# State-space layer: skip term by a diagonal matrix on TensorE, logarithm with the one as bias, second projection ahead of a round

## What is computed

```python
x = einsum('bld,ed->bel', hidden_states, in_proj_w)          # 4 x 256 channels x 256 tokens
x = silu(depthwise causal conv of 4 taps over x + conv_b)     # this is u
dt_low, Bm, Cm = split(einsum('bdl,ed->bel', x, x_proj_w), [8, 24])
dt = softplus(einsum('brl,dr->bdl', dt_low, dt_proj_w) + dt_proj_b)
A = -exp(A_log)                                               # 256 x 16
def step(state, d, b, c, u):                                  # along the tokens
    state = state * exp(d * A) + (d * u) * b
    y = einsum('bdn,bn->bd', state, c)
y = (y + D * x) * silu(z)                                     # D * x is the skip term
```

## Time and profile before

| | us |
|---|---|
| median of 3 runs | 1440.1 |
| lowest and highest of them | 1439.5, 1444.04 |
| time of the profiled execution | 1443.76 |
| its span, first to last instruction | 1442.0 |
| TensorE busy | 1310.5 (91%) |
| VectorE busy | 1019.6 (71%) |
| ScalarE busy | 706.4 (49%) |
| GpSimd busy | 272.7 (19%) |
| mean granted TensorE clock | 0.950 of full |

### The profile page before, as it was taken

How to read it: one execution, slowest core, us unless ns; L and a number is a source line. 1 busy time by engine, 2 the same in 40 slices (tenths; PEclk the granted TensorE clock), 3 DMA queues, 4 the chain that set the end, 5 groups by cost and what they waited for, 6 DMA issues and landing times.

```text
span 1442.0 us, 20925 instructions
## 1 busy us (share of the span) xinstructions
PE 1310.5 (91%) x6697; PEld 920.2 (64%) x6697; DVE 1019.6 (71%) x2264; ACT 706.4 (49%) x1825; POOL 272.7 (19%) x258
## 2 busy tenths in 40 slices
PE   7898699989996668999999789987999999989998
PEld 3455465663342355766776789976888888765555
DVE  6999877988986877778777522236666666667665
ACT  5797524444774847455554112225666666623110
POOL 0787310010000003222220371111111111201000
PEclk8899889999998879999999699998999999989999
DMA  6579600044502000010105488855222221101330
GB/s 224 169 252 318 206 2 0 0 74 76 89 10 85 0 0 1 1 37 1 37 1 146 168 314 309 305 191 191 74 73 73 74 78 66 36 1 48 82 92 29
DMA packets 83570, 141.80 MB, mean 98 GB/s; under 512 B 45606, under 2 KB 57327, under 8 KB 78528
## 3 DMA queue, kind: packets, MB, share of 16 engines
q1 hardware_dynamic: 80528, 134.44, 29.5%
q0 software_dynamic: 1872, 4.22, 0.8%
q10 hardware_dynamic: 1088, 2.10, 0.4%
HBM read 105.32 MB, written 26.37 MB: 91 GB/s over the span
## 4 chain that ended last, share of the span: by engine, by line
PE 74%; DVE 12%; ACT 5%; issue 3%; DMA 3%; POOL 2%; SPq 1%; DVEq 0%; POOLq 0%; ACTq 0%
PE psum L3363 5%; PE psum L2540 4%; PE psum L2106 4%; PE psum L2860 4%; PE psum L996 4%; PE psum L2912 4%; PE psum L2890 4%; PE psum L2148 4%; PE psum L2925 3%; PE psum L3373 3%; PE psum L603 2%; PE psum L537 2%; DVE roomB L1662 2%; PE psum L2138 2%; PE psum L2551 2%
## 5 line engine op out<-in xcount | busy, mean ns | idle before, releaser
L2982 ACT ACTIVATE roomA<-psum,roomA 128x256 f32<-128x256 f32 x128 | 70.9, 559 | 87.2 <-DVE roomA L3049 86.9
L2203 ACT ACTIVATE roomA<-psum,roomA 128x128 f32<-128x128 f32 (+1 forms) x128 | 53.2, 426 | 84.3 <-DVE roomA L2278 84.2
L1662 DVE TENSOR_REDUCE roomB<-psum 128x2 f32<-128x512 f32 x128 | 81.3, 685 | 10.5 <-PE psum L1501 10.0
L2711 DVE SCALAR_TENSOR_TENSOR roomA<-roomA,psum 128x512 f32<-128x512 f32 x23 | 15.9, 689 | 100.6 <-ACT roomA L2600 100.5
L2069 POOL TENSOR_TENSOR roomA<-roomA 128x512 f32<-128x512 f32 x40 | 51.1, 1279 | 176.6 <-DVE roomA L2271 176.6
L902 POOL TENSOR_TENSOR roomA<-roomA 128x1024 f32<-128x1024 f32 (+1 forms) x33 | 74.8, 2268 | 25.6 <-DVE roomA L822 24.9
L2106 PE MATMUL psum<-own,roomB 128*128 128x512 f32 x160 | 75.0, 594 | 3.4 <-DVE roomA L2270 2.1
L822 DVE TENSOR_TENSOR_SCAN roomA<-roomA,psum 128x512 f32<-128x512 f32 x64 | 74.3, 1200 | 0.9 <-ACT roomA L704 0.9
L3363 PE MATMUL psum<-roomA,roomB 128*112 128x512 f32 (+1 forms) x168 | 74.6, 593 | 0.0
L2912 PE MATMUL psum<-roomA 128*128 128x256 f32 x256 | 67.5, 386 | 1.7 <-ACT roomA L2990 0.7
L2890 PE MATMUL psum<-roomA 128*128 128x256 f32 x256 | 65.6, 379 | 1.7 <-ACT roomA L2982 1.7
(11 more groups left out here) (525 smaller groups left out, 3374.3 us busy)
## 6 DMA issues: line engine op xcount, KB each, us to landing
roomB<-m_w_dram SPq DMA_DIRECT2D x12, 1536.0 KB, 8.2
roomA<-m_w_dram SPq DMA_DIRECT2D x11, 1536.0 KB, 8.8
roomA<-m_c_rows SPq DMA_DIRECT2D x32, 512.0 KB, 4.6
a_kv_ready<-roomB SPq DMA_DIRECT2D x28, 512.0 KB, 5.3
roomA<-a_kv_ready SPq DMA_DIRECT2D x8, 1024.0 KB, 4.9
roomA<-a_kv_ready SPq DMA_DIRECT2D x16, 512.0 KB, 4.3
roomB<-a_w_dram SPq DMA_DIRECT2D x4, 1280.0 KB, 5.6
roomB<-f_w_dram SPq DMA_DIRECT2D x8, 624.0 KB, 4.3
```

The source lines that it names most:

```text
L1662: dve.tensor_reduce(maxneg[:, hp // 8, :, m, hp % 8], g.bank(m).rearrange("p (q k) -> p q k", k=S), AX.X, ALU.max, negate=True).then_inc(s ...
```

## The change

1. The skip term. Two 128x128 tiles `skips`, the identity times D, are made by VectorE at the start. `skip_over(j)` multiplies them with u on TensorE into banks 0 and 1, ahead of the first `add` of each half; the adds then all accumulate. `with_skip` is gone, `gate` reads PSUM, and for j = 0 both gates stand between product and scan of step 17.
2. The logarithm. `logarithm(j)` reads exp(-|v|) itself and takes a tile of ones as bias. `one_more(1)` goes from GpSimd to VectorE, at step 1 ahead of `remainder(1)`; `remainder(j)` now waits for the logarithm too, since it overwrites what that reads.
3. The order. `project(1)` stands ahead of round 4, whose halves stand behind it and behind `step_size(1)`. `kv_out(4)` moves from before the table load to behind `logarithm(1)`, ahead of `kv_out(5)`.

```diff
+        pool.memset(g.one, 1.0)
...
+    skips = ra.take(E2, P)
...
         project(0)
-        kv_round(4)
         pe.wait_ge(s["m_u"], 2)
         project(1).then_inc(s["m_dtlow_psum"], 1)
+        kv_round(4, range(0, 2))
         pe.wait_ge(s["m_kv_copied"], 4)
         pe.wait_ge(s["m_dtlow"], 1)
         step_size(0)
         pe.wait_ge(s["m_less"], 1)
         take_off(0)
         step_size(1)
+        kv_round(4, range(2, 4))
         take_off(1)
         for r in range(5, AHEAD):
             kv_round(r)
...
+        def skip_over(j):
+            pe.wait_ge(s["m_made"], 4)
+            pe.wait_ge(*((s["m_hc"], 1), (s["m_gated"], 1))[j])
+            for half in range(2):
+                pe.matmul(g.bank(Y_BANK + half), skips[:, j, :], u[:, j, half * HALF:(half + 1) * HALF],
+                          start=True, stop=False, skip_group_check=True)
+
         def add(k):
+            if k % NS == 0:
+                skip_over(k // NS)
             for half in range(2):
...
-                if k == NS:
-                    pe.wait_ge(s["m_gated"], 1)
                 pe.matmul(g.bank(Y_BANK + half), g.ident, hC[:, k % 2, half * HALF:(half + 1) * HALF],
-                          start=(k % NS == 0), stop=(k % NS == NS - 1), skip_group_check=True).then_inc(s["m_added"], 1)
+                          start=False, stop=(k % NS == NS - 1), skip_group_check=True).then_inc(s["m_added"], 1)
 
         def back(j):
-            pe.wait_ge(s["m_gated"], 2 + j)
+            pe.wait_ge(s["m_gated"], 1 + j)
...
         kv_out(3)
-        kv_out(4)
         act.preload_act_table_set(LN_EXP)
...
         def logarithm(j):
-            act.wait_ge(s["m_w"], j + 1)
-            act.activation(th[:, j, :], dtu[:, j, :], ACT.Ln).then_inc(s["m_ln"], 1)
+            act.wait_ge(s["m_e"], j + 1)
+            act.activation(th[:, j, :], e[:, j, :], ACT.Ln, bias=g.one).then_inc(s["m_ln"], 1)
...
         shrink(1)
         decay(1)
         logarithm(1)
+        kv_out(4)
         kv_out(AHEAD - 1)
...
+        for j in range(E2):
+            dve.tensor_scalar(skips[:, j, :], g.ident, skip[:, j:j + 1], None, ALU.mult).then_inc(s["m_made"], 1)
...
         def remainder(j):
             dve.wait_ge(s["m_w"], j + 1)
+            dve.wait_ge(s["m_ln"], j + 1)
...
-        def with_skip(j, half):
-            of = slice(half * HALF, (half + 1) * HALF)
+        def gate(j, half):
             dve.wait_ge(s["m_added"], 2 * NS * (j + 1) - 1 + half)
-            return dve.scalar_tensor_tensor(dtu[:, j, of], u[:, j, of], skip[:, j:j + 1], g.bank(Y_BANK + half), ALU.mult, ALU.add)
-
-        def gate(j, half):
-            y = by_seq(dtu[:, j, :])[:, 2 * half:2 * half + 2, :]
-            return dve.scalar_tensor_tensor(y, gates[:, 2 * half:2 * half + 2, j, :], 0.5, y, ALU.mult, ALU.mult)
+            y = g.bank(Y_BANK + half).rearrange("p (b l) -> p b l", b=2)
+            return dve.scalar_tensor_tensor(by_seq(dtu[:, j, :])[:, 2 * half:2 * half + 2, :], gates[:, 2 * half:2 * half + 2, j, :], 0.5, y,
+                                            ALU.mult, ALU.mult)
 
         for k in range(STEPS):
             inputs(k)
             if k == 1:
+                one_more(1)
                 remainder(1).then_inc(s["m_w"], 1)
             if k == NS + 1:
-                with_skip(0, 0)
-                with_skip(0, 1).then_inc(s["m_gated"], 1)
+                dve.wait_ge(s["m_gates"], 4)
+                gate(0, 0)
+                gate(0, 1).then_inc(s["m_gated"], 1)
             scan(k)
...
-            if k == NS + 2:
-                dve.wait_ge(s["m_gates"], 4)
-                dve.wait_ge(s["m_gated"], 1)
-                gate(0, 0)
-                gate(0, 1).then_inc(s["m_gated"], 1)
...
         for half in range(2):
-            step(with_skip(1, half))
             gate(1, half).then_inc(s["m_gated"], 1)
...
-        pool.wait_ge(s["m_e"], 2)
-        pool.tensor_scalar(dtu[:, 1, :], e[:, 1, :], 1.0, None, ALU.add).then_inc(s["m_w"], 1)
```

More of the change, by code:

```diff
@@ L600, in add @@
                     pe.wait_ge(s["m_hc"], k + 1 + (half if k == STEPS - 2 else k // (STEPS - 1)))
-                if k == NS:
-                    pe.wait_ge(s["m_gated"], 1)
                 pe.matmul(g.bank(Y_BANK + half), g.ident, hC[:, k % 2, half * HALF:(half + 1) * HALF],
-                          start=(k % NS == 0), stop=(k % NS == NS - 1), skip_group_check=True).then_inc(s["m_added"], 1)
+                          start=False, stop=(k % NS == NS - 1), skip_group_check=True).then_inc(s["m_added"], 1)
         def back(j):
-            pe.wait_ge(s["m_gated"], 2 + j)
+            pe.wait_ge(s["m_gated"], 1 + j)
             for i in range(NT):
                 if j and i == NT // 2:
-                    pe.wait_ge(s["m_gated"], 4)
+                    pe.wait_ge(s["m_gated"], 3)
                 b, r = i // 2, i % 2
@@ L653, in scalar @@
         act.activation(A, a_log, ACT.Exp).then_inc(s["m_aexp"], 1)
-        act.wait_ge(s["m_pad"], 2)
+        act.wait_ge(s["m_made"], 2)
         for b in range(4):
@@ L689, in scalar @@
         split(1)
-        act.wait_ge(s["m_u"], 2)
         logarithm(0)
@@ L728, in vector @@
         step = g.dve_steps
-        dve.memset(xpad[:, :, :, 0:TAPS - 1], 0.0).then_inc(s["m_pad"], 1)
+        dve.memset(xpad[:, :, :, 0:TAPS - 1], 0.0).then_inc(s["m_made"], 1)
         dve.wait_ge(s["ident"], 3)
@@ L733, in vector @@
         dve.tensor_copy(sel[0:96], ones[0:96, 0:NS].unsqueeze(2).to_broadcast([96, NS, P])).then_inc(s["m_sel"], 1)
-        dve.memset(by_seq(dA[1])[:, :, 0:1], 0.0).then_inc(s["m_pad"], 1)
+        dve.memset(by_seq(dA[1])[:, :, 0:1], 0.0).then_inc(s["m_made"], 1)
         dve.wait_ge(s["m_weights"], 48)
         step(dve.tensor_scalar(small[:, 0:10], small[:, 0:10], 0.5, None, ALU.mult))
+        for j in range(E2):
+            dve.tensor_scalar(skips[:, j, :], g.ident, skip[:, j:j + 1], None, ALU.mult).then_inc(s["m_made"], 1)
         def conv(j, k):
@@ L3646, in sb @@
             return Room(ctx.enter_context(nc.sbuf_tensor(name, [P, words], F32)), words)
-        own = sb("own", 2 * NT * D + KD * TOK + TOK + P + P // 2 + 240 + 256)
+        own = sb("own", 2 * NT * D + KD * TOK + TOK + P + P // 2 + 240 + 256 + 2)
         g.X = own.take(NT, D)
@@ L3661, in program @@
         g.var, g.rstd, g.t8a, g.t8b = (own.take(NT) for _ in range(4))
+        g.one = own.take(1)
         g.roomA = sb("roomA", 25600)
```

## The result

| | before | changed |
|---|---|---|
| median of the runs, us | 1440.26 (6 runs) | 1449.21 (6 runs) |
| lowest and highest, us | 1439.5, 1444.04 | 1447.72, 1452.9 |
| profiled execution, us | 1443.76 | 1447.72 |
| its span, us | 1442.0 | 1446.0 |

The ratio is 1.0065, 95% interval 1.0049 to 1.0081: the change makes the kernel slower by 9 us. The forecast was 1443.7, with a range up to 1447.5. Yet the two profiled executions lie 4.0 us apart, which is nearly the +3.6 of the forecast's sum. Both have to be explained.

The account below looks back on a forecast made before the run. VectorE was taken to pace the first layer's loop, TensorE close behind, after a TensorE-ScalarE prologue chain. 7.0 - 0.3 + 1.6 - 0.4 - 3.0 - 1.3 = +3.6 on median 1440.1 gave 1443.7 us, range 1438.5 to 1447.5.

Parts of the forecast that it names:

- first product at 47.3 instead of 40.3: Loop entry: VectorE's first product waits for round 4's deferred copy, round 5 and the first spread; loss 7.0 us.
- Second projection ahead of round 4: Prologue: projection starts at 22.45 instead of 23.50, dtlow copy at 24.45 instead of 25.93; 1.5 us gained there.
- Copy of round 4 behind the second logarithm, round 5, spread: Prologue: the chain the first product waits for; copy done at 43.0, round 5 from 43.05, first product 47.3.
- Logarithm with the one as bias: Prologue and step 1: remainder's wait hidden; second addition 0.7 us on VectorE, first product with C freed, gain 0.3.
- First skip pair: Ahead of the first add, partly at low clock: loss 1.6 us, of which 0.4 may be caught again.
- Gate of step 18 gone, end of the layer: Mid-loop a 3.43 us gate goes, gain 3.0; at the end two operations go, gain 1.3 us.
- the 0.4 that was to be caught again: First ten loop steps: half of a 0.85 us difference between ScalarE's and VectorE's delays regained, bounds 0 and 0.85.
- the clock staying up through the prologue: Rival: 2.4 GHz kept through the prologue, first product at 45.15, +4.8 instead of +7.0; 1441.5 us; chance 0.22.
- The C rows: Rival: C rows, queued behind round 4's store, reach GpSimd late, up to 1.5 us slip; 1445.2 us; chance 0.28.
- The chance of slower: Whole kernel: probability 0.37 that the change is measurably slower, against 0.53 within and 0.10 faster.
- The size of a measurable difference: Whole kernel: 0.3%, 4.3 us, taken as about what a measurement can tell from none.

Follow-up runs that it names:

- the order undone: Changed kernel with the second projection, round 4 and its copy back in the order of before; median 1440.69 us, ratio 0.9991.
- the skip term alone: Kernel before with only the skip term moved to TensorE and the gates reading PSUM; median 1441.76 us, ratio 0.9997.
- copy early: Changed kernel with ScalarE's copy of round 4 moved right behind the first logarithm; median 1440.44 us, ratio 0.9997.
- round 5 later: Changed kernel with round 5 moved behind the spread for step 1, copy of round 4 left in place; median 1450.43 us, ratio 1.0049.

## Why the prediction was wrong, step by step

**The step that failed** is the last of the sum: "The profiled execution took 1443.8 ... it lies 3.7 above the median of the three runs, and against the median 1440.1 the forecast is 1443.7". It carries a difference worked out in one execution over to the median, as if the 3.7 us lay outside the change's reach. They lay in it: by the traces 2.8 of them were the late first product (40.3 against 37.5), behind the late load of x, and the change takes out just that dependence. So the term "first product at 47.3 instead of 40.3" is not 7.0 but 9.8. Of the 2.8 the small copy's start is 1.5 (25.93 against 24.40), which the forecast booked as the projection's gain; the rest is that the first step sizes still ran at the full clock for a part or all of the way (2.55 and 1.95 us instead of 3.37), which it booked as the change's too. The forecast's other terms unchanged, the sum is then 9.8 - 0.3 + 1.6 - 0.4 - 3.0 - 1.3 = +6.4, near the 6.5 to 7.3 by which the adds to X move between the usual executions. The medians of the runs differ by 7.9 and 9.0 us; the cause of the last 0.6 to 2.5 us isn't shown.

Against the trace that it was made from the forecast held, in its parts too: spans +4.0 for +3.6, the first product 6.9 later for 7.0, 2.7 won back for 3.4, and the same time behind the adds to X (1275.8 against 1276.0).

Point by point:
- *Second projection ahead of round 4*: said 1.5 gained; measured 1.5 against the first trace, nothing against the usual one.
- *Copy of round 4 behind the second logarithm, round 5, spread*: right in every link, and shown by the copy moved and by the order undone.
- *Logarithm with the one as bias*: hidden, as said. The remainder began at 32.01 (31.9 said). The second addition took 1.95 instead of 0.7, and the remainder behind it 1.23 instead of 2.72. They ended at 55.05, 1.8 us behind GpSimd's end at 53.24, exactly the value taken from the row. By the Trainium skill (SBUF — State Buffer, section Who interferes with whom) the later operation is blocked fully, which would be 1.9: the trace agrees nearly, the blocked operation ended 0.55 us behind GpSimd's end, 0.14 less than its own 0.69.
- *First skip pair*: from first product to the copy of round 6 it was 14.6 instead of 12.8, 1.8 more, where 1.3 was said. The clock rose 5.2 us after the pair's start (53.38 to 58.6), not 4.7. But the pair itself was little of it: moved away, it gave back 0.6 and 0.9.
- *Gate of step 18 gone, end of the layer*: said 3.0 and 1.3. From the copy of round 6 to the adds to X it was 112.9, 113.7 and 112.9 us before and 108.4 in all three executions of the changed kernel: 4.5 to 5.3 less where these terms, with the 0.4 that was to be caught again, say 4.7. All that follows the first product was to give 3.4 and gave 2.7 in the first pair of traces, 2.5 to 3.1 against the other two. Most of the shortfall is at the loop's entry.
- *The rivals*: the clock staying up through the prologue was seen in one of three traces. The C rows bound nothing in two of three, and in the third GpSimd started 0.2 us behind the scan's end (48.62 against 46.08 + 2.33). The place was right, the price wasn't due, and with the spread free they cost all that this had won.
- *The chance of slower*, 0.37, was too low for the same reason as the number. *The size of a measurable difference*, 4.3 us, was too large: the interval of six runs against six reaches 0.16%, 2.3 us, to either side.

**Open.** The five versions in which neither the first spread nor the rows of C wait long for the copy of round 4, and the skip term alone, end the layer 1 to 4 us before the kernel before does, and by medians gain between nothing and 3. From the adds to X to the end of the span the profiled executions take between 1271.8 and 1280.6 us, over code that is the same in all. This goes with the clock: for the same matmuls there TensorE was busy 1159.9 us in the two shortest (1271.8 and 1273.9), 1164.5 to 1168.4 in the four longest (1279.0 to 1280.6), and 1161.6 to 1165.5 in the others. Over all executions the mean granted clock of the span was 0.956 at best (1435.16 us, copy early) and 0.938 at worst (1451.73, round 5 later). What makes the clock fall more in one execution than in another, and whether the changed order does, isn't shown. The changed kernel's mean clock is lower (medians 0.942 and 0.944, against 0.950 for the kernel before timed with the parts), but the layer itself, at the low clock from 28 to 58.6, is part of that.

## What to carry to other kernels

Where a term of the sum hangs on when a load or a clock change happens to fall, one trace is one draw: compare its time with the median, and look first for what in it was late, because a change may remove just that. A difference of two spans may not be added to a median of other executions. When work is deferred, follow all its consumers: the copy of a PSUM bank freed a bank on TensorE and a store in SyncE's queue, and two waits of equal length hide each other, so that an experiment that frees one shows nothing. Here the deferred copy belonged in the first gap of ScalarE behind its producer, not behind the chain that ends in the second logarithm.

## Not expected of the hardware

- TensorE's granted clock, over nearly the same matmuls, left 2.4 GHz in microseconds 26 to 28 in twelve of fourteen profiled executions, in 29 with the copy early, and in 30 in one execution of the changed kernel. There the copy of round 4 came 1.9 us earlier (39.95 against 41.86) and the first product 2.4 (44.87 against 47.22), the rest because the clock was up again from microsecond 44 on.
- A one-operand operation of 1024 elements on VectorE took 1.95 us instead of 0.69 beside GpSimd's product (51.84 against 50.89 to 53.24), and the two-operand one behind it its usual 1.23. With round 5 behind the spread, GpSimd's product only started at 51.45, and the same two, at 43.03 and 43.75, took 0.68 and 1.22.
